# Last stage of a four-layer transformer kernel: the layout of the sets' results and the grouping of the products with the permutation

## The reference, cut to what matters

```
grouped = x.reshape(b, s // g, g, d)                 # 64 groups of g = 32 tokens, d = 256
...
perm = (logits == max over the 32 tokens)            # per group and set: which token
permuted = einsum('bntd,bntes->bnesd', grouped, perm)
inner = relu(einsum('bnesd,esdf->bnesf', permuted, W1) + b1)      # 128 sets, f = 32
result_permuted = einsum('bnesf,esdf->bnesd', inner, W2) + b2
result = einsum('bnesd,bntes->bntd', result_permuted, perm)       # back to token order
```

## Time and profile before

| | us |
|---|---|
| median of 3 runs (977.0 to 981.29) | 977.71 |
| the profiled execution's own time | 980.43 |
| its span, first to last instruction | 978.6 |
| mean granted PE clock over the span (share of 2.4 GHz) | 0.875 |
| first `e1` matmul to the last `e2` read-out (892.30 to 932.28) | 40.0 |
| first transpose to the start of the last product with `perm` (932.34 to 974.92) | 42.6 |

### The profile page before, as it was taken

The page is one execution under the profiler, slowest core; times in us unless marked ns, Lnnn a source line. Parts: engine busy times, 40 slices in busy tenths (PEclk is TensorE's granted clock), DMA queues, the critical chain, the costliest instruction groups (busy, mean ns, idle before and its releaser), DMA issues.

```text
span 978.6 us, 16232 instructions
## 1 busy us (share of the span) xinstructions
PE 800.0 (82%) x6103; PEld 605.3 (62%) x6103; DVE 501.8 (51%) x1223; ACT 344.4 (35%) x627; POOL 242.9 (25%) x242
## 2 busy tenths in 40 slices
PE   3557989899999999831799999935479888997998
PEld 2335766566665665531699999924356666675865
DVE  3544577876778765422112212125556886444743
ACT  1323544544544544400222222203044456443211
POOL 1512333322234321211211111026234532112000
PEclk9768989999999999965799999978587799657999
DMA  4959465754463663328454566346835550332001
GB/s 150 122 70 190 81 90 72 96 78 79 67 141 63 74 132 126 130 86 129 148 200 163 185 189 171 103 106 77 105 70 78 88 83 25 121 155 88 1 33 54
DMA packets 66896, 103.29 MB, mean 106 GB/s; under 512 B 21614, under 2 KB 56942, under 8 KB 61662
## 3 DMA queue, kind: packets, MB, share of 16 engines
q1 hardware_dynamic: 64403, 97.07, 47.2%
q0 software_dynamic: 2416, 5.19, 2.9%
HBM read 56.61 MB, written 7.28 MB: 65 GB/s over the span
## 4 chain that ended last, share of the span: by engine, by line
PE 64%; DVE 11%; DMA 8%; ACT 5%; issue 4%; POOL 4%; SPq 3%; DVEq 0%; POOLq 0%; ACTq 0%
PE PS L724 9%; PE U L735 8%; PE U L641 7%; PE MB L574 6%; PE MB L662 5%; PE MB L652 4%; PE PS L627 4%; PE MB L604 4%; PE MB L804 3%; PE MB L590 3%; PE MB L814 2%; SPq L1460 2%; DMA y<-yb,pos 2%; DVE nma L1070 2%; DMA QKa<-mTa 2%
## 5 line engine op out<-in xcount | busy, mean ns | idle before, releaser
L1070 DVE TENSOR_REDUCE nma<-MB 128x2 f32<-128x512 f32 (+1 forms) x192 | 124.2, 672 | 40.5 <-PE MB L604 39.7
L900 ACT ACTIVATE Pa<-PS 128x1024 f32<-128x1024 f32 (+1 forms) x96 | 97.4, 1023 | 73.9 <-PE PS L627 73.0
L1305 POOL TENSOR_TENSOR mv<-mv,vec 128x2 f32<-128x2 f32 x48 | 34.7, 723 | 273.9 <-DVE mv L1025 273.8
L604 PE MATMUL MB<-QKa 99*128 99x120 bf16 (+1 forms) x512 | 73.8, 261 | 26.1 <-DVE nma L1070 14.1
L641 PE MATMUL U<-Pa,Vaa 128*32 128x256 f32 (+1 forms) x768 | 91.6, 401 | 0.9 <-ACT Pa L900 0.7
L724 PE MATMUL PS<-mzT,mw 128*128 128x128 f32 x736 | 87.7, 278 | 1.8 <-ACT mzT L921 1.8
L724 PEld LDWEIGHTS PS<-mzT,mw 128*128 128x128 f32 x736 | 85.7, 195 | 2.4 <-issue 2.3
L735 PE MATMUL U<-mw,mdT 128*128 x368 | 83.3, 379 | 2.3 <-DVE mdT L1209 2.3
L604 PEld LDWEIGHTS MB<-QKa 99*128 99x128 bf16 x512 | 40.7, 105 | 59.5 <-DVE nma L1070 21.8
L735 PEld LDWEIGHTS U<-mw,mdT 128*128 128x128 f32 x368 | 68.2, 190 | 11.0 <-issue 2.7
L1217 DVE TENSOR_TENSOR yt<-U,mb 128x256 f32<-128x256 f32 x23 | 9.8, 425 | 123.2 <-PE U L735 123.2
(11 more groups left out here) (194 smaller groups left out, 1442.8 us busy)
## 6 DMA issues: line engine op xcount, KB each, us to landing
mw<-in_mw SPq DMA_DIRECT2D x31, 1024.0 KB, 5.5
QKa<-spa SPq DMA_DIRECT2D x144, 128.0 KB, 5.1
Qb<-spb SPq DMA_DIRECT2D x48, 128.0 KB, 5.3
Oa<-Uba SPq DMA_DIRECT2D x16, 256.0 KB
v<-in_v SPq DMA_DIRECT2D x1, 4096.0 KB, 13.2
v<-in_v SPq DMA_DIRECT2D x4, 1024.0 KB, 11.2
W<-in_W SPq DMA_DIRECT2D x3, 1280.0 KB, 7.0
yb<-yt SPq DMA_DIRECT2D x23, 128.0 KB, 1.7
```

The costliest lines, as they stand in the source:

```text
L604: i = e.matmul(b[:, keys * j:keys * j + keys], Q[0:99, h0 + j, 128 * qt:128 * qt + 128], K[0:99, h0 + j, 0:keys], start=True, stop=True)
L900: e.activation(p[0:keys, :], ps[0:keys, :], ACT.Exp, scale=0.25).then_inc(sems["exp"], 1)
L1070: e.tensor_reduce(A.nm[qt][:, h0:h0 + heads], b[:, 0:heads * keys].rearrange("p (h s) -> p h s", h=heads), AX.X, ALU.max, negate=True).the ...
L1305: e.tensor_tensor(rs[r][:, 0:2], ve[r][:, 0:2], mhalf[:, 0:2], ALU.pow).then_inc(sems["rs"], 1)
```

## The change

`e2`'s read-out writes into a new tile `R` of shape [128, 2, 64, 128] = [feature, k, n, s] on the same memory as `G`. Since it overlies inputs that `e1` still reads, all four `e1` come before the first `e2`; `Tmp` becomes a ring of 4. The transposes read `R[:, k, 2m + n, :]`. `Yn` becomes a ring of 4 in another area, `tu` comes in pairs, and one `cm`(t) does the four products of what were `cm`(2t) and `cm`(2t + 1).

```diff
-    out += [("ex",), ("e1", 0)]
-    for b in range(4):
-        if b + 1 < 4:
-            out.append(("e1", b + 1))
-        out += [("e2", b, q) for q in range(8)]
-    out.append(("tu", 0))
-    for m in range(32):
-        if m + 1 < 32:
-            out.append(("tu", m + 1))
-        out.append(("cm", m))
+    out += [("ex",)] + [("e1", b) for b in range(4)]
+    out += [("e2", b, q) for b in range(4) for q in range(8)]
+    out += [("tu", 0), ("tu", 1)]
+    for t in range(NT):
+        if t + 1 < NT:
+            out += [("tu", 2 * t + 2), ("tu", 2 * t + 3)]
+        out.append(("cm", t))
...
+    R = Area(r_at).new("R", [128, 2, 64, 128])
+    Yn = Area(s_at).ring("Yn", 4, [128, 2, 256])
...
-                    i = e.transpose(b[:, 256 * n + 128 * k:256 * n + 128 * k + 128], G[:, k, :, 2 * m + n], idf[:, :])
+                    i = e.transpose(b[:, 256 * n + 128 * k:256 * n + 128 * k + 128], R[:, k, 2 * m + n, :], idf[:, :])
...
+        def combine(t):
+            ps = pair("cm", t)
+            g.wait_ge("turned_a", t + 1)
+            g.wait_ge("turned_b", t + 1)
+            for signal in PAIRS.free["cm", t] or ():
+                g.free(signal)
+            for j in range(4):
+                m, n = 2 * t + j // 2, j % 2
+                i = e.matmul(ps[32 * j:32 * j + 32, 0:256], perm[:, 2 * m + n, :], Yn[m % 4][:, n, :], start=True, stop=True)
             i.then_inc(sems["comb"], 1)
...
 (VectorE, bias of the first and of the second products)
-            g.wait_ge("relu", b - 1)
...
+            g.wait_ge("e1", 4)
             g.wait_ge("e2", 8 * b + q + 1)
-            e.tensor_tensor(G[:, :, s:s + 4, :], bank("e2", b, q)[:, :].rearrange("p (k s n) -> p k s n", k=2, s=4),
+            e.tensor_tensor(R[:, :, :, s:s + 4].rearrange("p k n s -> p k s n"), bank("e2", b, q)[:, :].rearrange("p (k s n) -> p k s n", k=2, s=4),
...
 (ScalarE and VectorE, copies into Yn)
-                g.wait_ge("comb", m - 1)
+                g.wait_ge("comb", m // 2 - 1)
```

More of the change, by code:

```diff
@@ L245, in score_users @@
             yield s, (("sorted_a" if key[1] == 0 else "sorted_b", 2 * key[0] + 2),)
-        elif what == "cm" and key[0] % 2 == 0:
-            yield s, (("added", key[0] // 2 + 1),)
+        elif what == "cm":
+            yield s, (("added", key[0] + 1),)
 PAIRS = Ring(2, score_users())
@@ L469, in build @@
     c2 = ta.new("c2", [128, 2, 128])
-    Tmp = ta.ring("etmp", 2, [128, 8, 64])
-    Yn = ta.ring("Yn", 2, [128, 2, 256])
+    Tmp = ta.ring("etmp", 4, [128, 8, 64])
+    R = Area(r_at).new("R", [128, 2, 64, 128])
+    Yn = Area(s_at).ring("Yn", 4, [128, 2, 256])
     names = ("idb va delta tb na nb split_m v_done max_done mh recip o_scaled resid gate rank cnt rows_of own mid_b "
@@ L965, in sets_up @@
             for j in range(4):
-                i = e.activation(BD[b % 2][32 * j:32 * j + 32, :, j, :], Tmp[b % 2][32 * j:32 * j + 32, :, :], ACT.Relu)
+                i = e.activation(BD[b % 2][32 * j:32 * j + 32, :, j, :], Tmp[b][32 * j:32 * j + 32, :, :], ACT.Relu)
             i.then_inc(sems["relu"], 1)
@@ L970, in turn @@
             if m % 2 == 0:
-                g.wait_ge("comb", m - 1)
+                g.wait_ge("p2", 24)
+                g.wait_ge("comb", m // 2 - 1)
                 g.wait_ge("turn", m + 1)
-                e.activation(Yn[m % 2][:, :, :], bank("tu", m)[:, :].rearrange("p (n d) -> p n d", n=2),
+                e.activation(Yn[m % 4][:, :, :], bank("tu", m)[:, :].rearrange("p (n d) -> p n d", n=2),
                              ACT.Identity).then_inc(sems["turned_a"], 1)
@@ L1251, in sets_up @@
             g.wait_ge("offset", 24)
-            g.wait_ge("relu", b - 1)
             g.wait_ge("e1", b + 1)
-            e.tensor_tensor(Tmp[b % 2][:, :, :], bank("e1", b)[:, :].rearrange("p (q n) -> p q n", q=8),
+            e.tensor_tensor(Tmp[b][:, :, :], bank("e1", b)[:, :].rearrange("p (q n) -> p q n", q=8),
                             over(vec[:, V_BM1 + 8 * b:V_BM1 + 8 * b + 8], 64, 2), ALU.add).then_inc(sems["up"], 1)
@@ L1265, in turn, with combine @@
             if m % 2:
-                g.wait_ge("comb", m - 1)
+                g.wait_ge("comb", m // 2 - 1)
                 g.wait_ge("turn", m + 1)
-                e.tensor_copy(Yn[m % 2][:, :, :], bank("tu", m)[:, :].rearrange("p (n d) -> p n d", n=2)
+                e.tensor_copy(Yn[m % 4][:, :, :], bank("tu", m)[:, :].rearrange("p (n d) -> p n d", n=2)
                               ).then_inc(sems["turned_b"], 1)
[L1271 to L1275, removed]
+        def combine(t):
+            g.wait_ge("comb", t + 1)
+            e.tensor_tensor(x[:, t, :], x[:, t, :], pair("cm", t)[:, 0:256], ALU.add).then_inc(sems["added"], 1)
         does = {"in": copy_in, "a0": lambda: ones_and_delta(AA, "a"), "a2": second_attention, "tb": query_bias,
@@ L1556, in last_weights, with combine @@
                 e.dma_start(v2[:, 8 * b:8 * b + 8, :], D["v2"][:, 8 * b:8 * b + 8, :]).then_inc(sems[f"d_v2{b}"], 16)
-        def combine(m):
-            t = m // 2
-            if m % 4 == 3:
+        def combine(t):
+            if t % 2:
                 g.wait_ge("added", t + 1)
```

## The result

Timed beside each other, 13 runs each: 968.12 us after, 978.78 before, ratio 0.9893 (95% interval 0.9872 to 0.9915). That is 10.7 us faster, where 19.0 were forecast, and 2 us above the top of the range. The same kernel, timed twice more, gave 0.9853 (0.9824 to 0.9882) and 0.9871 (0.9834 to 0.9908), 12.5 and 13.0 us between the medians; the first of these had a median of 964.25 us, which lies inside the range, but its profile has the same stops as the others, so that number doesn't bear out the forecast. The profiled execution took 966.02 us with a span of 964.2, where the sum had 959.6. Single runs of either kernel spread over some 9 us, and in its three profiles the changed kernel reaches the first `e1` 1.2 us earlier than the one profile of before, over unchanged code; so what follows is read from stages of the profiles.

The account below looks back on a forecast made before the run. PE was taken to bound both late stages. -1.0 us (`e1` order and strided read-outs) and -18.0 us (transposes and products) gave -19.0, so 977.7 becomes 958.7 us; range 956 to 966.

Parts of the forecast that it names:

- the sum: Whole kernel: -1.0 - 18.0 = -19.0 us; span 978.6 becomes 959.6, median 977.7 becomes 958.7 us.
- Step 1: All `e1` before `e2`: two more cost 2 x 1.99 us, first `e2` at about 901.45, its read-out 902.6 instead of 900.51.
- Step 2: `e2`'s read-outs write with 512-byte steps: 0.89 us per read-out; with the new `e1` order, first transpose 1.0 us earlier.
- full price: `e2`'s strided read-outs don't overlap: 1.05 us each, +3.9 instead of -1.0, 963.6 us; chance 0.14.
- a costlier 512-byte step: `e2`'s read-outs: longer pitch; at twice 0.865, about 985.6 us; chance 0.05 above 1.49 us, 0.07 between 1.1 and 1.49.
- Steps 3 and 4: Contiguous transposes, 1.00 us per eight for 1.56; products in four column groups, 0.57 per tile for 1.12; together -18.0 us.
- The two rivals on PE: Transposes don't get faster, 965.1 us, chance 0.05; the products' four strips don't run together, 967.5 us, chance 0.03.
- Step 5: Transposes and products: read-outs, banks and transfers don't come between PE's blocks; costed at nothing in a 1.57 us period.
- The prediction's last sentence: Second products, or transposes and products: a granted clock below 1.00 in either stage would make all of it wrong.

Follow-up runs that it names:

- late load: The changed kernel, with the 2 MB of weights for sets 32 to 95 asked for only after all four `e1`: 964.25 us, 0.9837 of the kernel before.
- experiment 5: The late load with `e1`'s operands read as bf16, 128 instead of 256 instructions per `e1`: 958.9 us, 0.9803 of the kernel before.
- experiments 1 and 2: The changed kernel without the last 2 MB of weights (other sets' weights used): 964.36 us; and the late load: 964.25 us; each 0.9837 of the kernel before.

## Why the prediction was wrong, point by point

*Step 1, all e1 first* failed. It took 1.99 us for each further `e1`, the distance measured for one `e1` behind eight `e2`, and the gap before the first `e2` as free time for them. Between the old `e1`(1) and `e1`(2) lie 32 slow matmuls that let the supply catch up; in a row, the third and fourth take some 3.5 us each (3.46 to 3.74 with idle DMA), what 256 instructions take to come. Measured: 14.7 us to the first `e2` instead of 9.15, an error of 5.5. Of it 2.0 are the weight transfer (late load; some 0.4 of that is `e1`(3) at the lower clock that followed the longer gap), 2.8 to 3.1 the two gaps of supply, and some 0.4 that the first two `e1` and the change-over took longer. The prediction said that the number of instructions stays and went by durations alone; how fast they arrive was in no term and no rival. The unknown that the range lacked was a bound on this term: I gave it one price and no spread.

*Step 2, the strided write*, was right with its numbers: 0.88 us apart for 0.89, 1.03 long for 1.02. Both of its rivals, full price and a costlier 512-byte step, are refuted by the profile. That the first of them stood at 963.6 us, near what later runs measured, is a coincidence: the time went elsewhere. The rule of 16-byte lines in the Trainium skill, page "SBUF — State Buffer", section "Specifications (TRN2)", agrees in kind (1.03 against 0.69 us for a write in one piece); that a longer step costs no more is shown for 256 and 512 bytes only.

*Steps 3 and 4* were right: 1.02 and 0.57 us for 1.00 and 0.57, 141 ns for 142; alone, the grouping gave 1.95 us for 1.97. Together 25.2 us for 24.6, so -17.4 for -18.0; 0.2 of the difference is the first four `tu` (2.06 for 1.87), the rest 0.02 in each block. The two rivals on PE are refuted.

*Step 5* was right: no read-out stands between those blocks. The prediction's last sentence, on the clock, was half right: it fell, but in `e1`(2) and `e1`(3), behind the stop; it was 1.00 in the `e2` and in the transposes and products.

*The sum*, in the profile: 959.6 + 5.5 (step 1) + 0.6 (steps 3 and 4) - 1.2 (earlier start of the stage) - 0.3 (read-outs at 0.88) = 964.2, which is the span. The medians stand 10.7, 12.5 and 13.0 us apart in the three timings, the stage alone 13.2 ((978.6 - 892.30) - (964.2 - 891.11)). Why the first timing shows less than the stage I can't say; its interval reaches to 12.5.

## What to carry to other kernels

When steps of many short matmuls are put next to each other, count the instructions and not only the durations: here PE got 256 instructions per 3.5 us and could use them in 2.0. A distance between two steps holds for their neighbours of that moment; long matmuls between short ones were cover for the instruction supply, and the order took it away. And a large transfer is best not asked for just before such a row: here it cost 2.0 us.

## What the runs showed of the hardware

- PE's instructions come in packets of 256 (49 for 12,206, two fewer for 512 fewer), one every 3.4 to 3.6 us when PE waits for them, 5.4 us when 2 MB of weights came between. The stops lie after 139 (0.4 us at most at full length), 267 and 395 matmuls, 256 instructions apart. That these packets are PE's is shown by experiment 5; that they are what PE waits for is inferred from the counts, from the places of the stops and from the times; no view names the wait. Whether 3.46 us is a delay for each packet or a rate is not separated.
- The Trainium skill, page "Advanced Engine Details and Errata", section "ISA Cache", says that a line of this cache holds 256 instructions and that there are two. The distance of 256 agrees, and so does that no more than the block in use and the next seem to be there. It also gives TensorE 128 KB, four times the others. By its 256 instructions for 16 KB that would be 2048, an estimate; with that much in store, no stop would be expected after 278 instructions, where experiment 5 has one of 1.67 us. I had not weighed this page. It has no rate; the 3.46 us is from the runs.
- DVE's float32 writes with 512-byte steps last 1.03 us for 512 elements but start 0.88 apart, though each has a wait of its own (the changed kernel, line 1262).
- Stops of 3.1 to 3.9 us were followed by a lower granted clock, 0.56 to 0.68 on the mean of the next `e1` (four profiles); behind stops of 1.4 to 1.7 us it stayed at 1.00 (experiments 1 and 2), and in experiment 5 it was 0.50 before and behind the stop.
